# Seven accumulating transfers a head, and score tiles in sets of two and three, in a fused attention layer

## The chip, the cores and the metric

The kernel runs on one core of a Trainium2 chip. The metric is the device time of one execution in microseconds (us). All data are float32, held in HBM at the start and at the end.

## The reference

A layer norm feeds two branches whose results are added to the input: multi-head attention with biases, and three matrix products followed by a tanh. There are 4 sequences of 2048 tokens and 512 channels; attention has 16 heads of 32 channels, so 64 (sequence, head) pairs, called heads here.

```python
B, S, DIM, H = 4, 2048, 512, 16
def attention(xn):
    q = split_heads(xn @ q_w.T + q_b, H) / sqrt(DIM // H)
    k = split_heads(xn @ k_w.T + k_b, H)
    v = split_heads(xn @ v_w.T + v_b, H)
    attn = softmax(einsum('bhqd,bhkd->bhqk', q, k))      # 2048 x 2048 per head
    ctx = merge_heads(einsum('bhqk,bhkd->bhqd', attn, v))
    return ctx @ out_w.T + out_b
def ffn(xn):
    return tanh(xn @ weight @ aux_weight1 @ aux_weight2 + ffn_bias)
out = x + attention(layernorm(x)) + ffn(layernorm(x))
```

## The kernel before

**Stages.** `build_weights` and `build_project` prepare and project the tokens and leave q, k (each split in a high and a low part), v and the tanh branch in HBM. `build_attend` runs the 64 heads one after another, in a loop of four heads a turn whose last four heads are written out, and then the output projection. The change is in `build_attend` alone.

**One head on TensorE (PE).** The scores of a head are computed twice. The first time (`max_scores`, into `sm_bank`, line 926) they give the row maxima: 64 units, each a 128 x 512 block. The second time (`scores`, into `st_bank`, line 942) they are laid out keys by queries, with the maximum folded in as an extra row: 16 key tiles `kt`, each 128 x 2048 and in four units. `both_scores` interleaves the two unit by unit, the maxima belonging to the next head: tile `kt` goes with the maxima units 4(kt+4) to 4(kt+4)+3 of the next head, and tiles 12 to 15 with the units 0 to 15 of the head after that. `use` multiplies a finished tile of probabilities with v (`pv_bank`, line 948), four matmuls a tile. The order is written out by hand in pairs of tiles: scores of tiles 2p and 2p+1, then `use` of the pair before. `turn_max` (line 935) transposes the 16 columns of maxima and stands before unit 8, that is before tile 14. `add_up` (also line 948, into `sm_bank`) sums the head's probability total over its partitions with a matrix of ones. It is written after the scores of tile 9 of the next head, and waits until all of that head's transfers into `dma_sum` have landed.

**Banks.** The maxima have 4 PSUM banks and the `st_bank` scores 3, so PE can be four maxima units ahead of VectorE (DVE) and three score units ahead of ScalarE (ACT). `st_slot` leaves a place out before units 22 (tile 5) and 44 (tile 11): these two wait for the unit two before them.

**ACT** takes the exponential of every score unit (`exps`, line 762) into one of eight `probs` buffers, tile 0 straight into `dma_sum`; it also copies `pv_bank` and the sums (line 769) and issues the next loads of q, k and v.

**DVE** reduces every maxima unit (line 846), turns the transposed maxima round (line 828), reduces the 64 partial maxima (line 863) and takes the reciprocal of the sums of the head before in pieces (line 838), placed after the maxima units named in `RECIPS`.

**GpSimd (POOL)** adds up probability tiles. Nine of its instructions a head (`add`, line 697) sum the ten tiles 1, 3, 4, 6, 7, 9, 11, 12, 14, 15 into `pool_sum`. The tiles 2, 5, 8, 10 and 13 are added onto tile 0 in `dma_sum` by accumulating DMAs that POOL issues (`join`, line 708), each of which waits until the one before has landed. A sixth one (`merge`, line 716) adds `pool_sum` to `dma_sum`. `scale` (line 722) multiplies the context by the reciprocals. POOL's order for a head is written by hand: join of tile 2, the first add, then the merge of the head before, the other adds with the joins of tiles 5, 8, 10 and 13 behind the adds 1, 3, 5 and 7, then `scale` of the head before, and the ninth add.

In the texts below "join 2" is the join of tile 2, and so on, and "sums" is PE's `add_up`.

Of the kernel before, what the change touches and what calls it, by code (L numbers as in the profile page):

```python
# [40 lines left out]
RECIPS = [63, 7, 15]  # L41
CUT = 10
LOAD_AT = [6, 7, 9, 10, 12, 13, 15]
# [4 lines left out]
POOL_TILES = [kt for kt in range(KT) if not any(kt in tiles for tiles in CHAINS)]  # L48
# [4 lines left out]
SCALE_ADD = 8  # L53
# [467 lines left out]
def build_attend(nc, dram, out, first):  # L521

    with ExitStack() as own:
# [27 lines left out]
        join_due, joined = sem("join_due"), [sem("joined0"), sem("joined1")]  # L553
        pool_added, sums_ready, recip_ready, context_ready = sem("pool_added"), sem("sums_ready"), sem("recip_ready"), sem("context_ready")
# [121 lines left out]
        def _(pool):  # L676
# [33 lines left out]

            def merge(h, r):

                pool.wait_ge(pool_added, PRIME + h * POOL_ADDS + POOL_ADDS)
                pool.wait_ge(joined[r % 2], landed(h, len(CHAINS[0]) - 1))
                pool.sem_inc(join_due, 1)
                nc.gpsimd.dma_start(dma_sum[r % 2][:], pool_sum[r % 2][:], accum_op=ALU.add).then_inc(joined[r % 2], DMA)
# [14 lines left out]
            for i in range(POOL_ADDS):  # L731
                sum_up(0, 0, i)

            def body(h, r, more, following):
                for i in range(POOL_ADDS):
                    if i == SCALE_ADD:
                        scale(h, r)
                    if more >= 1:
                        sum_up(following, (r + 1) % GROUP, i)
                    if i == MERGE_AFTER:  # L740
                        merge(h, r)

# [3 lines left out]
        def _(act):  # L746
# [3 lines left out]
            def exps(h, r, kt):  # L750

                for q in range(QB):
                    if q == 0 and kt in SLOT:
                        old, back = tile_before(kt)
                        act.wait_ge(tile_used, PRIME + h * KT - back * KT + old + 1)
                        if old in POOL_TILES:
                            act.wait_ge(pool_added, PRIME + h * POOL_ADDS - back * POOL_ADDS + adds_after(old))
                        elif old != kt and not (back and isinstance(h, int) and h == 0):
                            before, place = (h - 1, (r + 1) % 2) if back else (h, r % 2)
                            act.wait_ge(joined[place], landed(before, CHAINS[0].index(old)))  # L760
# [148 lines left out]
        def _(pe):  # L909
# [79 lines left out]
            for p in range(CUT // 2):  # L989
                both_scores(0, 0, 2 * p, 1, 2)  # L990
                both_scores(0, 0, 2 * p + 1, 1, 2)
                if p:
                    use(0, 0, 2 * p - 2)
                    use(0, 0, 2 * p - 1)

            def body(h, r, more, following, to_turn):
                r1 = (r + 1) % GROUP
                for p in range(CUT // 2, KT // 2):
                    both_scores(h, r, 2 * p, to_turn, more)
                    both_scores(h, r, 2 * p + 1, to_turn, more)  # L1000
                    use(h, r, 2 * p - 2)
                    use(h, r, 2 * p - 1)
                if more >= 1:
                    for p in range(CUT // 2):
                        both_scores(following, r1, 2 * p, to_turn + 1, more - 1)
                        both_scores(following, r1, 2 * p + 1, to_turn + 1, more - 1)
                        if p == 0:
                            use(h, r, KT - 2)
                            use(h, r, KT - 1)
                        else:  # L1010
                            use(following, r1, 2 * p - 2)
                            use(following, r1, 2 * p - 1)
                        if p == CUT // 2 - 1:
                            add_up(h, r, more)
                else:
                    use(h, r, KT - 2)
                    use(h, r, KT - 1)
# [72 lines left out]
```

## Time and profile before

| | us |
|---|---|
| median of 3 runs (lowest, highest) | 4178.22 (4175.97, 4180.62) |
| the profiled execution, its own time | 4178.57 |
| its span in the trace | 4176.8 |
| PE busy | 4086.4 (98%) |
| POOL busy | 3251.6 (78%) |
| DVE busy | 3110.1 (74%) |
| ACT busy | 2360.6 (57%) |
| `scale` of the first head starts | 948.2 |
| `scale` of the last head starts | 4006.9 |

The share of the whole span says little, since the heads are only the part from about 900 to 4010 us. PE, POOL and the DMA engines all have to be read there, head by head. Matmuls are pipelined, and the profile models their ends: a busy PE need not be a PE at its peak, so its time is read from the distance of the starts.

### The profile page before, as it was taken

The page shows a single profiled execution, that of the slowest core. Times are in us where ns is not written, and L with a number is a line of the kernel's source. Part 1 is how long each engine was busy: PE and PEld are TensorE (multiplying, and loading weights), DVE is VectorE, ACT ScalarE, POOL GpSimd, SP SyncE. Part 2 cuts the span into 40 slices and gives each one's busy share as a digit, 9 for nine tenths or more (in the row PEclk, how much of TensorE's full clock was granted, in tenths as well). Part 3 has the DMA queues.
Part 4 walks back from the last instruction along what each step waited for, and adds up shares of the span by engine and source line. Part 5 has one row for each costly group of instructions (what it writes and reads, how often), then busy time and mean ns, then how long its engine had stood idle before and what let it go on. Part 6 is the DMA issues. An engine that isn't in the chain of part 4 may idle for free.

```text
span 4176.8 us, 77708 instructions
## 1 busy us (share of the span) xinstructions
PE 4086.4 (98%) x21216; PEld 2490.0 (60%) x21216; DVE 3110.1 (74%) x5056; ACT 2360.6 (57%) x4517; POOL 3251.6 (78%) x1183
## 2 busy tenths in 40 slices
PE   8999999899999999999999999999999999999989
PEld 6888888655555555555555555555555555555467
DVE  4443334588888888888888888888888888888444
ACT  2221222166666666666666666666666667666621
POOL 1222222279999999999999999999999999999920
PEclk9999999999999999999999999999999999999999
DMA  4444445368788888888888888888888888887777
GB/s 169 163 162 158 151 161 170 132 139 170 166 177 175 179 170 174 171 173 172 175 177 173 175 171 167 172 175 177 176 171 172 173 173 175 176 178 163 167 248 250
DMA packets 246256, 722.11 MB, mean 173 GB/s; under 512 B 87296, under 2 KB 88320, under 8 KB 184448
## 3 DMA queue, kind: packets, MB, share of 16 engines
q0 software_dynamic: 55296, 402.68, 49.8%
q1 hardware_dynamic: 107552, 201.88, 14.2%
q10 hardware_dynamic: 83040, 113.01, 9.7%
q8 instruction: 185, 3.03, 0.3%
q14 instruction: 183, 1.50, 0.1%
HBM read 178.00 MB, written 136.31 MB: 75 GB/s over the span
## 4 chain that ended last, share of the span: by engine, by line
PE 48%; DMA 18%; issue 9%; ACT 3%; POOL 2%; POOLq 0%; DVE 0%; ACTq 0%; SPq 0%; DVEq 0%
PE sm_bank L926 14%; PE st_bank L942 14%; PE pv_bank L948 14%; DMA dma_sum<-pool_sum 10%; DMA dma_sum<-probs 7%; PE sm_bank L235 3%; ACT probs L762 3%; PE sm_bank L948 1%; POOL pool_sum L697 1%; PE st_bank L235 1%; POOL ctx_out L722 1%; POOL dma_sum L708 0%; PE sm_bank L935 0%; ACTq L761 0%; DMA k_stack<-s_k_hi 0%
## 5 line engine op out<-in xcount | busy, mean ns | idle before, releaser
L846 DVE TENSOR_REDUCE part_max<-sm_bank 128x1 f32<-128x512 f32 x4032 | 2450.4, 677 | 413.8 <-PE sm_bank L926 407.4
L697 POOL TENSOR_TENSOR pool_sum<-pool_sum,probs 128x2048 f32<-128x2048 f32 x512 | 2503.2, 4889 | 18.1 <-ACT probs L762 2.2
L762 ACT ACTIVATE probs<-st_bank 128x512 f32<-128x512 f32 x3840 | 1959.3, 614 | 610.5 <-PE st_bank L942 577.7
L926 PE MATMUL sm_bank<-k_stack,q_stack 96*128 96x512 f32 x4032 | 1663.0, 413 | 4.4 <-issue 2.7
L942 PE MATMUL st_bank<-q_stack,k_stack 97*128 97x512 f32 x4096 | 1647.1, 403 | 14.8 <-ACT probs L762 8.5
L926 PEld LDWEIGHTS sm_bank<-k_stack,q_stack 96*128 96x128 f32 x4032 | 767.2, 190 | 558.8 <-DVE part_max L846 339.0
L942 PEld LDWEIGHTS st_bank<-q_stack,k_stack 97*128 97x128 f32 x4096 | 778.6, 190 | 271.4 <-ACT probs L762 127.6
L948 PE MATMUL pv_bank<-probs,v_pair 128*32 128x512 f32 x7680 | 937.6, 603 | 0.0
L948 PEld LDWEIGHTS pv_bank<-probs,v_pair 128*32 128x32 f32 x7680 | 204.9, 109 | 457.3 <-ACT probs L762 264.0
L708 POOL DMA_DIRECT2D dma_sum<-probs x320 | 349.3, 1092 | 80.3 <-ACT probs L762 35.2
L349 POOL TENSOR_TENSOR y_out<-y_out,x_in 128x512 f32<-128x512 f32 x64 | 82.7, 1292 | 385.7 <-ACT y_out L378 379.9
L697 POOL TENSOR_TENSOR pool_sum<-probs 128x2048 f32<-128x2048 f32 x64 | 330.5, 5164 | 0.1
L838 DVE RECIPROCAL ratio<-sum_copy 128x168 f32<-128x168 f32 (+1 forms) x192 | 230.5, 1202 | 42.3 <-ACT sum_copy L769 42.3
L372 ACT ACTIVATE qk_hi<-proj,qk_bias 128x512 fp32r<-128x512 f32 x128 | 88.3, 690 | 271.3 <-PE proj L235 271.3
L431 DVE SCALAR_TENSOR_TENSOR qk_lo<-proj,qk_bias,qk_hi 128x512 fp32r<-128x512 f32 x128 | 96.1, 751 | 194.8 <-ACT qk_hi L372 193.0
L378 ACT ACTIVATE y_out<-y_out 128x512 f32<-128x512 f32 x64 | 40.5, 633 | 333.0 <-DVE y_out L457 333.0
L762 ACT ACTIVATE dma_sum<-st_bank 128x512 f32<-128x512 f32 x256 | 132.5, 602 | 146.5 <-PE st_bank L942 146.5
L235 PE MATMUL proj<-xt_hi,w_hi 128*128 128x512 f32 x512 | 202.9, 396 | 2.2 <-DVEq L461 2.2
L235 PE MATMUL proj<-w_hi,xt_lo 128*128 128x512 f32 x512 | 204.0, 398 | 0.0
L235 PE MATMUL proj<-xt_hi,w_lo 128*128 128x512 f32 x512 | 203.0, 396 | 0.0
L235 PE MATMUL proj<-xt_lo,w_hi 128*128 128x512 f32 x512 | 202.8, 396 | 0.0
L235 PE MATMUL proj<-w_hi,xt_hi 128*128 128x512 f32 x512 | 202.3, 395 | 0.0
(100 smaller groups left out, 2401.6 us busy)
## 6 DMA issues: line engine op xcount, KB each, us to landing
dma_sum<-probs POOLq DMA_DIRECT2D x320, 1024.0 KB, 8.3
dma_sum<-pool_sum POOLq DMA_DIRECT2D x64, 1024.0 KB, 10.3
q_stack<-s_q_hi ACTq DMA_DIRECT2D x122, 256.0 KB, 5.6
k_stack<-s_k_hi ACTq DMA_DIRECT2D x122, 256.0 KB, 4.4
x_in<-in_x SPq DMA_DIRECT2D x16, 1024.0 KB, 7.7
s_q_hi<-qk_hi SPq DMA_DIRECT2D x16, 1024.0 KB, 4.3
s_q_lo<-qk_lo SPq DMA_DIRECT2D x16, 1024.0 KB, 6.5
s_k_hi<-qk_hi SPq DMA_DIRECT2D x16, 1024.0 KB, 4.3
```

Of the source, the lines that this page charges most:

```text
L235: last = nc.tensor.matmul(out, a(c), b(c), start=(c == 0 and n == 0), stop=(c == CT - 1 and n == 2))
L349: nc.gpsimd.tensor_tensor(y_out[:, j], y_out[:, j], x_in[par][:, j], ALU.add).then_inc(half_y, 1)
L372: nc.scalar.activation(qk_hi[:, t, g], proj[:, u % RING], ACT.Identity, bias=keep["qk_bias"][:, t, g:g + 1]).then_inc(hi_ready, 1)
L431: nc.vector.scalar_tensor_tensor(qk_lo[:, t, g], proj[:, u % RING], keep["qk_bias"][:, t, g:g + 1], qk_hi[:, t, g].bitcast(F32), ALU.add, ...
L697: nc.gpsimd.tensor_tensor(total[:], one[:], tile_at(r, kt)[:], ALU.add).then_inc(pool_added, 1)
L708: nc.gpsimd.dma_start(dma_sum[r % 2][:], tile_at(r, CHAINS[0][j])[:], accum_op=ALU.add).then_inc(joined[r % 2], DMA)
L762: nc.scalar.activation(tile_at(r, kt)[:, q * BLK:(q + 1) * BLK], st_bank[:, st_place(kt * QB + q)], ACT.Exp, scale=SCALE).then_inc(probs_r ...
L838: nc.vector.reciprocal(ratio[:, columns], sum_copy[r % 2][:, columns]).then_inc(recip_ready, 1)
L846: nc.vector.tensor_reduce(part_max[:, k:k + 1], sm_bank[:, sm_place(k)], AX.X, ALU.max).then_inc(max_scores_read, 1)
L926: nc.tensor.matmul(sm_bank[:, sm_place(k)], q_st[r][0:ROWS, q * P:(q + 1) * P], k_st[r][0:ROWS, b * BLK:(b + 1) * BLK], start=True, stop=T ...
L942: nc.tensor.matmul(st_bank[:, st_place(u)], k_st[r][0:ROWS + 1, kt * P:(kt + 1) * P], q_st[r][0:ROWS + 1, q * BLK:(q + 1) * BLK], start=Tr ...
L948: last = nc.tensor.matmul(bank[q * DH:(q + 1) * DH, :], left, right[:, q * BLK:(q + 1) * BLK], start=start, stop=stop)
```

## The change

- **The last tile.** Tile 15 is no longer among POOL's tiles, so there are eight adds a head. In its place `top_up` issues an accumulating DMA of tile 15 onto `pool_sum`, with semaphores of its own (`topped`), once the head's adds are done and the tile is there. `merge` waits for `topped` and not for the last add. ACT waits for `topped` before it fills the buffer of tile 15 again, with tile 7 of the next head.
- **POOL's order.** `scale` stands behind all adds of the next head, and `top_up` of the next head behind `scale`.
- **PE's order.** Six sets of 2, 2, 3, 3, 3, 3 tiles in place of eight pairs; `add_up` is still behind the scores of tile 9. `turn_max` now falls inside the last set.
- **The reciprocal** in two pieces of 256 columns, behind the maxima units 3 and 15, in place of three of 168, 168 and 176 behind 63, 7 and 15.

```diff
-RECIPS = [63, 7, 15]
+RECIPS = [3, 15]
+SETS = [(0, 1), (2, 3), (4, 5, 6), (7, 8, 9), (10, 11, 12), (13, 14, 15)]
+CUT_SET = 4
...
-POOL_TILES = [kt for kt in range(KT) if not any(kt in tiles for tiles in CHAINS)]
+TOP = KT - 1
+POOL_TILES = [kt for kt in range(TOP) if not any(kt in tiles for tiles in CHAINS)]
...
+            def top_up(h, r):
+
+                pool.wait_ge(probs_ready, PRIME + h * UNITS + QB * (TOP + 1))
+                pool.wait_ge(pool_added, PRIME + h * POOL_ADDS + POOL_ADDS)
+                pool.sem_inc(join_due, 1)
+                nc.gpsimd.dma_start(pool_sum[r % 2][:], tile_at(r, TOP)[:], accum_op=ALU.add).then_inc(topped[r % 2], DMA)
+
             def merge(h, r):
 
-                pool.wait_ge(pool_added, PRIME + h * POOL_ADDS + POOL_ADDS)
+                pool.wait_ge(topped[r % 2], (h // 2) * DMA + DMA)
                 pool.wait_ge(joined[r % 2], landed(h, len(CHAINS[0]) - 1))
...
             def body(h, r, more, following):
                 for i in range(POOL_ADDS):
-                    if i == SCALE_ADD:
-                        scale(h, r)
                     if more >= 1:
                         sum_up(following, (r + 1) % GROUP, i)
                     if i == MERGE_AFTER:
                         merge(h, r)
+                scale(h, r)
+                if more >= 1:
+                    top_up(following, (r + 1) % GROUP)
...
+                        elif old == TOP and not (isinstance(h, int) and h == 0):
+                            act.wait_ge(topped[(r + 1) % 2], ((h - 1) // 2) * DMA + DMA)
...
             def body(h, r, more, following, to_turn):
                 r1 = (r + 1) % GROUP
-                for p in range(CUT // 2, KT // 2):
-                    both_scores(h, r, 2 * p, to_turn, more)
-                    both_scores(h, r, 2 * p + 1, to_turn, more)
-                    use(h, r, 2 * p - 2)
-                    use(h, r, 2 * p - 1)
+                for g in range(CUT_SET, len(SETS)):
+                    for kt in SETS[g]:
+                        both_scores(h, r, kt, to_turn, more)
+                    for kt in SETS[g - 1]:
+                        use(h, r, kt)
                 if more >= 1:
-                    for p in range(CUT // 2):
...
+                    for g in range(CUT_SET):
+                        for kt in SETS[g]:
+                            both_scores(following, r1, kt, to_turn + 1, more - 1)
+                        for kt in SETS[g - 1]:
+                            use(following if g else h, r1 if g else r, kt)
+                    add_up(h, r, more)
```

On POOL, from the join of tile 13 of one head to the join of tile 5 of the next, before:

```order
L708 DMA dma_sum<-probs 128x2048
...
L722 TENSOR_TENSOR ctx_out<-pv_copy,ratio 128x512
...
L697 TENSOR_TENSOR pool_sum<-pool_sum,probs 128x2048
...
L708 DMA dma_sum<-probs 128x2048
...
L697 TENSOR_TENSOR pool_sum<-probs 128x2048
...
L716 DMA dma_sum<-pool_sum 128x2048
...
L697 TENSOR_TENSOR pool_sum<-pool_sum,probs 128x2048
...
L708 DMA dma_sum<-probs 128x2048
```

And the same stretch now:

```order
L712 DMA dma_sum<-probs 128x2048
...
L733 TENSOR_TENSOR ctx_out<-pv_copy,ratio 128x512
...
L720 DMA pool_sum<-probs 128x2048
...
L712 DMA dma_sum<-probs 128x2048
...
L701 TENSOR_TENSOR pool_sum<-probs 128x2048
...
L727 DMA dma_sum<-pool_sum 128x2048
...
L701 TENSOR_TENSOR pool_sum<-pool_sum,probs 128x2048
...
L712 DMA dma_sum<-probs 128x2048
```

Where an add of about one tile stood between join 13 and join 2, there is now only the issue of a transfer (L720), and what the merge (L727) waits for has become that transfer.

On PE, in the last head, which has no maxima beside its scores (a tile of scores is four matmuls, and so is a `use`), from tile 4 on. Before:

```order
L942 MATMUL st_bank<-q_stack,k_stack 128x512 x8
L948 MATMUL pv_bank<-probs,v_pair 32x512 x8
L948 MATMUL sm_bank<-dma_sum,ones_att 32x512 x4
L942 MATMUL st_bank<-q_stack,k_stack 128x512 x8
L948 MATMUL pv_bank<-probs,v_pair 32x512 x8
```

Now:

```order
L957 MATMUL st_bank<-q_stack,k_stack 128x512 x12
L963 MATMUL pv_bank<-probs,v_pair 32x512 x12
L963 MATMUL sm_bank<-dma_sum,ones_att 32x512 x4
L957 MATMUL st_bank<-q_stack,k_stack 128x512 x12
L963 MATMUL pv_bank<-probs,v_pair 32x512 x12
```

The sums stay where they were; around them PE changes between scores and `use` after twelve matmuls where it did after eight.

On DVE, in the head before the last, from its maxima unit 16 to the end of what accompanies tile 15. Before:

```order
L846 TENSOR_REDUCE part_max<-sm_bank 128x1 x48
L838 RECIPROCAL ratio<-sum_copy 128x168
L863 TENSOR_REDUCE row_max<-part_max 128x16
L846 TENSOR_REDUCE part_max<-sm_bank 128x1 x8
L838 RECIPROCAL ratio<-sum_copy 128x168
L828 TENSOR_SCALAR max_row<-sm_bank 16x128
L846 TENSOR_REDUCE part_max<-sm_bank 128x1 x8
L838 RECIPROCAL ratio<-sum_copy 128x176
```

Now:

```order
L861 TENSOR_REDUCE part_max<-sm_bank 128x1 x48
L878 TENSOR_REDUCE row_max<-part_max 128x16
L861 TENSOR_REDUCE part_max<-sm_bank 128x1 x4
L853 RECIPROCAL ratio<-sum_copy 128x256
L861 TENSOR_REDUCE part_max<-sm_bank 128x1 x4
L843 TENSOR_SCALAR max_row<-sm_bank 16x128
L861 TENSOR_REDUCE part_max<-sm_bank 128x1 x8
L853 RECIPROCAL ratio<-sum_copy 128x256
```

The two pieces stand where the sets (10, 11, 12) and (13, 14, 15) end, and `max_row` has twelve reductions around it with no change of PE to `use` between.

## Rows read from the trace of the kernel before

**Rows 1.** The page: busy time by engine, DMA share in 40 slices.

```profile
PE 4086.4 (98%) x21216; PEld 2490.0 (60%) x21216; DVE 3110.1 (74%) x5056; ACT 2360.6 (57%) x4517; POOL 3251.6 (78%) x1183
DMA  4444445368788888888888888888888888887777
```

**Rows 2.** POOL's timeline (start us, us, engine, line), one head and its surroundings.

```profile
2413.66 0.89 POOL L708 DMA_DIRECT2D dma_sum<-probs  x1
2414.28 1.59 POOL L722 TENSOR_TENSOR ctx_out<-pv_copy,ratio 128x512 f32<-128x512 f32 x1
2415.54 4.88 POOL L697 TENSOR_TENSOR pool_sum<-pool_sum,probs 128x2048 f32<-128x2048 f32 x1
2420.08 1.19 POOL L708 DMA_DIRECT2D dma_sum<-probs  x1
2420.70 5.20 POOL L697 TENSOR_TENSOR pool_sum<-probs 128x2048 f32<-128x2048 f32 x1
2425.22 1.52 POOL L716 DMA_DIRECT2D dma_sum<-pool_sum  x1
2430.51 1.70 POOL L708 DMA_DIRECT2D dma_sum<-probs  x1
...
2442.19 0.88 POOL L708 DMA_DIRECT2D dma_sum<-probs  x1 [0.72 <-ACT probs L762]
...
2462.86 0.88 POOL L708 DMA_DIRECT2D dma_sum<-probs  x1 [0.37 <-ACT probs L762]
```

**Rows 3.** DMA issues of 2413 to 2421 us: count, KB, us to landing.

```profile
dma_sum<-probs POOLq DMA_DIRECT2D x2, 1024.0 KB, 7.4
```

**Rows 4.** The same of 2425.0 to 2426.5 us.

```profile
dma_sum<-pool_sum POOLq DMA_DIRECT2D x1, 1024.0 KB, 10.9
```

**Rows 5.** The same of 2430.3 to 2431.5 us.

```profile
dma_sum<-probs POOLq DMA_DIRECT2D x1, 1024.0 KB, 11.1
```

**Rows 6.** DMA of 2405 to 2454 us: GB/s in 40 slices of 1.225 us.

```profile
GB/s 214 214 214 214 0 13 0 0 207 221 214 214 166 162 214 214 214 181 234 221 221 201 227 274 227 214 140 301 54 207 13 107 214 214 214 107 294 139 1 107
```

**Rows 7.** Scale on POOL over all heads: duration ns, first and last start.

```profile
L722 POOL TENSOR_TENSOR ctx_out<-pv_copy,ratio x64: 1540/1578/3152, 948.2 to 4006.9; 128x512 f32<-128x512 f32 x64
```

**Rows 8.** PE's timeline: a change to use, one back, and the sums.

```profile
2408.86 0.40 PE L942 MATMUL st_bank<-q_stack,k_stack 97*128 97x512 f32 x1
2409.10 0.47 PE L926 MATMUL sm_bank<-k_stack,q_stack 96*128 96x512 f32 x1
2409.41 0.39 PE L942 MATMUL st_bank<-q_stack,k_stack 97*128 97x512 f32 x1
2409.73 1.92 PE L948 MATMUL pv_bank<-probs,v_pair 128*32 128x512 f32 x16
2411.58 0.50 PE L926 MATMUL sm_bank<-k_stack,q_stack 96*128 96x512 f32 x1
2411.92 0.40 PE L942 MATMUL st_bank<-q_stack,k_stack 97*128 97x512 f32 x1
...
2433.33 1.92 PE L948 MATMUL pv_bank<-probs,v_pair 128*32 128x512 f32 x16
2436.20 1.07 PE L948 MATMUL sm_bank<-dma_sum,ones_att 128*32 128x512 f32 x8 [0.94 <-DMA dma_sum<-pool_sum]
2437.19 0.50 PE L926 MATMUL sm_bank<-k_stack,q_stack 96*128 96x512 f32 x1
```

**Rows 9.** DVE's timeline: reductions, and the pieces of the reciprocal.

```profile
2399.42 1.19 DVE L838 RECIPROCAL ratio<-sum_copy 128x168 f32<-128x168 f32 x1
2400.53 0.22 DVE L828 TENSOR_SCALAR max_row<-sm_bank 16x128 fp32r<-16x128 f32 x1
2400.67 4.85 DVE L846 TENSOR_REDUCE part_max<-sm_bank 128x1 f32<-128x512 f32 x8
2405.45 1.23 DVE L838 RECIPROCAL ratio<-sum_copy 128x176 f32<-128x176 f32 x1
2412.12 4.87 DVE L846 TENSOR_REDUCE part_max<-sm_bank 128x1 f32<-128x512 f32 x8 [0.72 <-PE sm_bank L926]
```

More of the change, by code:

```diff
@@ L52 @@
 SLOT = {kt: i % 7 for i, kt in enumerate([*range(1, 13), 14, 15])} | {13: 7}
-SCALE_ADD = 8
 RESULT_TILES = [9, 11]
@@ L553, in build_attend @@
         join_due, joined = sem("join_due"), [sem("joined0"), sem("joined1")]
+        topped = [sem("topped0"), sem("topped1")]
         pool_added, sums_ready, recip_ready, context_ready = sem("pool_added"), sem("sums_ready"), sem("recip_ready"), sem("context_ready")
@@ L732, in _ @@
                 sum_up(0, 0, i)
+            top_up(0, 0)
             def body(h, r, more, following):
                 for i in range(POOL_ADDS):
-                    if i == SCALE_ADD:
-                        scale(h, r)
                     if more >= 1:
@@ L988, in _ @@
                 max_scores(1, 1, k)
-            for p in range(CUT // 2):
[L990 to L994, printed above, removed]
+            for g in range(CUT_SET):
+                for kt in SETS[g]:
+                    both_scores(0, 0, kt, 1, 2)
+                for kt in SETS[g - 1] if g else ():
+                    use(0, 0, kt)
             def body(h, r, more, following, to_turn):
                 r1 = (r + 1) % GROUP
-                for p in range(CUT // 2, KT // 2):
-                    both_scores(h, r, 2 * p, to_turn, more)
-                    both_scores(h, r, 2 * p + 1, to_turn, more)
-                    use(h, r, 2 * p - 2)
-                    use(h, r, 2 * p - 1)
-                if more >= 1:
[L1004 to L1014, printed above, removed]
-                else:
-                    use(h, r, KT - 2)
-                    use(h, r, KT - 1)
+                for g in range(CUT_SET, len(SETS)):
[3 more added lines that the diff above has]
+                        use(h, r, kt)
+                if more >= 1:
+                    for g in range(CUT_SET):
+                        for kt in SETS[g]:
+                            both_scores(following, r1, kt, to_turn + 1, more - 1)
+                        for kt in SETS[g - 1]:
+                            use(following if g else h, r1 if g else r, kt)
+                    add_up(h, r, more)
+                else:
+                    for kt in SETS[-1]:
+                        use(h, r, kt)
             def output(n, par, ahead):
```

## The prediction

> **What bounds the kernel now.** Start with the page's busy shares and the DMA line [rows 1]: PE at 98% looks like the bound, but in the heads, from the tenth slice on, the DMA engines are busy for 70 to 80% and more as well. The share does not tell which of them sets the length of a head. POOL's timeline does [rows 2]. Call J the issue of join 13 (2413.66). Then come the last add at J+1.88, join 2 at J+6.42, the merge at J+11.56, join 5 at J+16.85, join 8 at J+28.53 and, with join 10 between, the next join 13 20.67 later: 49.20 us for the head. POOL stands idle in only two places, 0.72 before join 8 and 0.37 before the next join 13, so 48.11 of the 49.20 is POOL's own work. The mean head is (4006.9 - 948.2) / 63 = 48.55 us [rows 7].
>
> The 0.72 is ascribed to ACT, but join 5 was issued at 2430.51 and landed 11.1 later, at 2441.61 [rows 5], and join 8, which must wait for it, followed 0.58 later. The reader is to see that the loop is POOL's work plus one DMA wait. Leaving the 0.37 out, the same sum for this head is 48.83, so it runs 0.28 above the mean, and I compare with 48.83.
>
> PE is second, and close: its use of the pair before the sums begins at 2433.33 and takes 1.85, so it could begin the sums at 2435.18 and begins at 2436.20, the moment when the merge lands (2425.22 + 10.9) [rows 4, 8]. PE needs 49.20 - 1.02 = 48.2 us in this head.
>
> **POOL's work.** One add goes: 2415.54 to 2420.08 is 4.54. One DMA issue comes: 0.62 (2413.66 to 2414.28) to 0.95 (the merge and join 5 stand before adds that end late); 0.7 taken. POOL's own work falls from 48.1 to about 44.3. Moving scale behind the adds costs nothing: it stood behind join 13 before, and stands there now. If nothing else changed, the head would be PE's.
>
> **The new wait.** The merge waited for an add that had ended nearly 5 us before. Now it waits for the seventh transfer, and this is issued at J+1.88, only 1.88 after join 13. Joins 13 and 2, the pair nearest to it, are 6.42 apart and land 7.4 after issue, each as good as alone [rows 2, 3]. Transfers of this kind do not overlap: one alone moves for four slices at 214 GB/s, 4.9 us, with pauses between them; closer ones run on at 200 to 230 GB/s without a pause [rows 6]. The three that are issued 5 us apart land at 2427.48, 2436.12 and 2441.61, 8.64 and 5.49 apart [rows 2 to 5], though nothing but bandwidth ties them. So the seventh lands about 4.9 after join 13: J + 7.4 + 4.9 = J+12.3, which is **10.4 after its own issue**. The ends: 7.4, as if alone, and 14.2, if it takes the merge's 8.64 behind join 13's landing. I take 10.4 because the stores of the context, which follow scale in both kernels, are already in the 7.4 of rows 3.
>
> In the meantime POOL issues join 2 (J+2.6) and does one add (4.52), until J+7.8. Then it waits for the seventh until T = J+12.3: **4.5 us idle**, on the engine that bounds the loop, with six more adds queued behind it.
>
> **The second wait grows.** The merge is issued at T+0.6 (the 0.58 between join 5's landing and join 8) and join 5 5.29 later, at T+5.9. Join 2 was issued long before, but its bytes only start when the seventh's end; it lands at T+4.9. If the merge and join 5 land 8.64 and 5.49 behind it, as now, join 8 can go at T+19.6. If nothing queued, POOL's work alone would bring it at T + 5.9 + 10.96 = T+16.9. I take 18.9, nearer to the first, since it is the same transfers and loads of q and k that compete; the slices in which the merge moves go down to 140 and 54 GB/s, so not all of its 8.64 is queue.
>
> **Sum of the loop.** 1.88 (join 13 and scale) + 10.4 (seventh) + 18.9 (to join 8) + 20.3 (20.67 less the 0.37) = **51.5 us**, against 48.83: +2.7. In the loop's 63 distances the first has no full queue, so 62 x 2.7 = +167.
>
> **PE's order.** Two changes between scores and use go. One costs 0.32 - 0.24 going in, 1.85 - 2 x 0.86 = 0.13 inside (a tile is 0.86, the two of 1.85 less the one of the sums, 0.99), and 0.34 - 0.24 coming back [rows 8]: 0.31, so -0.62 a head. Against it stands the ring of four maxima banks. In a set PE writes a maxima unit every 0.47 and DVE reads one in 0.60 (2400.67 to 2405.45, eight), starting 0.54 behind [rows 8, 9]. Unit k waits for the end of unit k-4, which is at 0.54 + 0.60 (k - 3) + 0.1; PE reaches it at 0.1 + 0.47 k. In pairs (k up to 7) it just holds; in threes, k = 11 is 0.2 late, 0.3 with the restart. This falls on (7, 8, 9). In (4, 5, 6) and (10, 11, 12) the units 22 and 44 hold PE anyway, which covers it. In (13, 14, 15) the larger piece of the reciprocal (256/168 x 1.11 = 1.7) makes DVE start some 0.3 later (12 x 0.60 + 1.7 = 8.9, against PE's 24 x 0.235 + 0.3 + 2.7 = 8.6), and max_row lies between: 0.7. Less 0.1 that pairs lose today, +0.9 at most, +0.7 taken. PE needs 48.2 - 0.6 + 0.7 = 48.3, with both ends 47.9 and 48.6. All of it hides under POOL's 51.5 and costs nothing, as long as the loop is POOL's. The reciprocal's pieces are 3.4 us in all either way and wait for sums that are ready a set of tiles earlier.
>
> ACT's new wait, for tile 7 on the seventh transfer, lies ahead of the sums of the same head. If it comes to anything it takes a part of PE's wait there and adds none: POOL waits for the same landing.
>
> **Total.** Against the profiled execution's own 4178.6 (span 4176.8; the median is 4178.2, so nothing is to be corrected): 4178.6 + 167 = 4346.
>
> **Rivals.**
> 1. *The transfers overlap, and PE sets the length: faster.* If the seventh lands 7.4 after issue and join 5 is no longer waited for, the loop is 1.88 + 7.4 + 16.9 + 20.3 = 46.5, PE's 48.3 is longer, and it gains 48.55 - 48.3 = 0.25, up to 0.65 a head: -15 to -40, 4155. It holds as soon as the seventh's latency and the 16.9 to 19.6 sum to under 26; I have 29.3. For it: POOL is truly relieved by 3.8 us. Against it: the flat 200 to 230 GB/s.
> The Trainium skill, "DMA: Bandwidth & Descriptors", section "Anatomy of one DMA — SWDGE (gpsimd) path", gives 2.0 us plus the bytes at 436 GB/s. By that, an estimate, the seventh would land under 5 us after its issue and this rival would hold. The trace disagrees: 7.4 for 1 MB alone.
> 2. *Only the first wait comes.* Seventh 10.4, but join 5 lands in time: 49.5, +0.7 a head, 4220; spread 4175 to 4265. For it: the merge's 8.64 contains loads that could fall elsewhere.
> 3. *The queue backs up further.* Seventh at 14.2: 55 and more, above 4440. Against it: nothing in the stretch before join 2 moves much but the 256 KB of stores.
>
> **How the numbers follow.** The forecast's own spread is a loop of 50.2 to 53.0, that is +1.4 to +4.2, 4265 to 4439: chance 0.71. Rival 1: 0.12. Rival 2: 0.12. Rival 3: 0.05. Range 4185 to 4440: it leaves out rival 1, rival 3 and the bottom of rival 2. Within 0.2% (8 us, about what a measurement can tell) lie 0.02 of rival 1 and 0.02 of rival 2: 0.04. Faster: 0.10 of rival 1 and 0.01 of rival 2, 0.11. Slower: 0.85.
>
> **What would show it.** In POOL's timeline after: the merge 12 to 13 us behind join 13's issue with some 4.5 idle before it; join 8 over 12.5 behind join 5, with an idle time that a DMA ends. In the DMA issues: the seventh landing at 10 to 11, join 5 at 12 or more. On PE: a wait of 2 to 3.5 before the sums in every head. It is wrong if POOL waits for ACT's tiles rather than for DMAs, if the seventh lands in under 8, or if PE's wait at the sums is gone.

## The result and the profile after

The changed kernel takes 4473.9 us (median of 4 runs, 4472.9 to 4475.6) against 4179.4 for the kernel before in the same runs: ratio 1.0709, 95% interval 1.0695 to 1.0722. It is slower by 294 us, or 4.7 us for each of the 63 steps from head to head. The direction was forecast, the size was not: 4346 was predicted, and the range ended at 4440. Some executions of any of these kernels ran slow as a whole; a kernel's time in this text is the median of the others.

Busy time by engine, and the DMA share in 40 slices, from the page of the changed kernel, beside [rows 1]:

```profile
PE 4196.0 (94%) x21216; PEld 2517.7 (56%) x21216; DVE 3130.0 (70%) x4992; ACT 2386.2 (53%) x4517; POOL 3015.3 (67%) x1183
DMA  4444445488888888888888888888888888888787
```

POOL does 236 us less and PE is idle more. What became longer is a wait. POOL's timeline of the changed kernel, from join 13 to the next one (start us, us, engine, line, idle before), beside [rows 2]:

```profile
2450.17 0.85 POOL L712 DMA_DIRECT2D dma_sum<-probs  x1
2450.78 1.56 POOL L733 TENSOR_TENSOR ctx_out<-pv_copy,ratio 128x512 f32<-128x512 f32 x1
2452.01 1.19 POOL L720 DMA_DIRECT2D pool_sum<-probs  x1
2454.75 0.87 POOL L712 DMA_DIRECT2D dma_sum<-probs  x1 [1.55 <-PE pv_bank L963]
2455.32 4.91 POOL L701 TENSOR_TENSOR pool_sum<-probs 128x2048 f32<-128x2048 f32 x1
2464.70 0.88 POOL L727 DMA_DIRECT2D dma_sum<-pool_sum  x1 [4.46 <-DMA pool_sum<-probs]
2465.32 4.88 POOL L701 TENSOR_TENSOR pool_sum<-pool_sum,probs 128x2048 f32<-128x2048 f32 x1
2470.68 0.88 POOL L712 DMA_DIRECT2D dma_sum<-probs  x1 [0.48 <-issue]
2471.30 9.47 POOL L701 TENSOR_TENSOR pool_sum<-pool_sum,probs 128x2048 f32<-128x2048 f32 x2
2483.17 0.88 POOL L712 DMA_DIRECT2D dma_sum<-probs  x1 [2.40 <-ACT probs L777]
...
2493.30 0.89 POOL L712 DMA_DIRECT2D dma_sum<-probs  x1
...
2503.39 0.88 POOL L712 DMA_DIRECT2D dma_sum<-probs  x1
```

Where POOL had two short waits in this stretch of its loop, 0.72 and 0.37, it now has four: before join 2 (1.55), before the merge (4.46, for the seventh transfer), before join 5 (0.48) and before join 8 (2.40). When the transfers issued at 2450.17, 2452.01, 2454.75, 2464.70 and 2470.68 landed is in five answers on the DMA issues of these moments, in this order (the last column is us from issue to landing), beside [rows 3 to 5]:

```profile
dma_sum<-probs POOLq DMA_DIRECT2D x1, 1024.0 KB, 8.4
pool_sum<-probs POOLq DMA_DIRECT2D x1, 1024.0 KB, 12.0
dma_sum<-probs POOLq DMA_DIRECT2D x1, 1024.0 KB, 15.4
dma_sum<-pool_sum POOLq DMA_DIRECT2D x1, 1024.0 KB, 12.7
dma_sum<-probs POOLq DMA_DIRECT2D x1, 1024.0 KB, 11.9
```

So they land at 2458.6, 2464.0, 2470.2, 2477.4 and 2482.6: one every 5 to 7 us, though the first three were issued within 5 us. The seventh, at 2464.0, lets the merge go at 2464.7. Join 2, at 2470.2, lets join 5 go at 2470.7; the profile calls this wait "issue", but join 5 may not go before join 2 has landed. Join 5, at 2482.6, lets join 8 go at 2483.2; the profile names ACT there, but in the mean too join 8 goes 0.6 after join 5 has landed.

This is one head. POOL's waits over all heads (us in total, times, longest) show the same places with another split: in the mean 3.5 us before join 2, for PE's use of tile 0, and 2.5 before the merge.

```profile
POOL dma_sum L712 <- PE pv_bank L963: 217.7, 62, 7.1
POOL dma_sum L727 <- DMA pool_sum<-probs: 149.3, 50, 12.3
```

The same distances, averaged over 60 heads of each trace (worked out from POOL's timeline and the DMA issues, us; predicted in the last column):

| from | to | before | after | predicted |
|---|---|---|---|---|
| join 13 | merge | 11.55 | 14.49 | 12.9 |
| merge | join 5 | 5.28 | 6.46 | 5.3 |
| join 5 | join 8 | 11.59 | 12.16 | 13.0 |
| join 8 | next join 13 | 20.38 | 20.37 | 20.3 |
| **a head** | | **48.80** | **53.48** | **51.5** |
| issue to landing | join 13 | 7.6 | 7.6 | 7.4 |
| | seventh | | 11.8 | 10.4 |
| | join 2 | 7.9 | 13.7 | |
| | merge | 10.2 | 12.6 | |
| | join 5 | 11.0 | 11.6 | |

63 times 4.68 is 295 us, the whole result. PE waits for POOL's loop before the sums, 2.1 us each time in 57 heads:

```profile
PE sm_bank L963 <- DMA dma_sum<-pool_sum: 120.4, 57, 6.5
```

(who waited for whom on PE: us in total, times, longest). There is a second wait on PE's side. ACT's tile 9 takes the `probs` buffer of tile 2, and so waits until join 2 has landed:

```profile
2470.22 1.58 ACT L777 ACTIVATE probs<-st_bank 128x512 f32<-128x512 f32 x3 [2.04 <-DMA dma_sum<-probs]
```

With ACT held, the scores of the set (7, 8, 9) take PE 1.3 us longer in the mean than in e4 below, where nothing of the kind is waited for. Both waits lie within what PE has to spare. TensorE's granted clock in the heads falls from 1.00 to 0.97 or 0.98 of 2.4 GHz in the windows of 500 us, with PE waiting more. A set without such a wait is no longer for it ((13, 14, 15) is 6.31 us here and in e4), so I take the clock for a follower; no run holds it fixed.

### The profile page after: what moved, and what is told of

It is laid out like the page before. It is cut to its first block and busy times, and to the rows that moved or that the text cites. A ratio compares the mean times of both kernels' runs of the same rounds, so it can differ in the third digit from the quotient of the medians.

```text
span 4473.8 us, 77764 instructions
## 1 busy us (share of the span) xinstructions
PE 4196.0 (94%) x21216; PEld 2517.7 (56%) x21216; DVE 3130.0 (70%) x4992; ACT 2386.2 (53%) x4517; POOL 3015.3 (67%) x1183
## 5 line engine op out<-in xcount | busy, mean ns | idle before, releaser
L777 ACT ACTIVATE probs<-st_bank 128x512 f32<-128x512 f32 x3840 | 1985.5, 610 | 584.2 <-PE st_bank L957 465.4
L701 POOL TENSOR_TENSOR pool_sum<-pool_sum,probs 128x2048 f32<-128x2048 f32 x448 | 2131.4, 4758 | 16.8 <-ACT probs L777 1.0
L957 PE MATMUL st_bank<-q_stack,k_stack 97*128 97x512 f32 x4096 | 1677.7, 411 | 85.2 <-ACT probs L777 77.7
L941 PE MATMUL sm_bank<-k_stack,q_stack 96*128 96x512 f32 x4032 | 1717.1, 427 | 26.7 <-DVE part_max L861 25.4
L957 PEld LDWEIGHTS st_bank<-q_stack,k_stack 97*128 97x128 f32 x4096 | 794.6, 194 | 348.2 <-ACT probs L777 207.9
L963 PE MATMUL pv_bank<-probs,v_pair 128*32 128x512 f32 x7680 | 932.5, 614 | 0.0
L712 POOL DMA_DIRECT2D dma_sum<-probs x320 | 284.6, 889 | 448.9 <-PE pv_bank L963 250.7
L963 PEld LDWEIGHTS pv_bank<-probs,v_pair 128*32 128x32 f32 x7680 | 221.7, 112 | 515.4 <-issue 291.1
L701 POOL TENSOR_TENSOR pool_sum<-probs 128x2048 f32<-128x2048 f32 x64 | 314.8, 4918 | 4.5 <-ACT probs L777 4.4
L853 DVE RECIPROCAL ratio<-sum_copy 128x256 f32<-128x256 f32 x128 | 222.1, 1736 | 48.8 <-ACT sum_copy L784 48.8
L784 ACT ACTIVATE sum_copy<-sm_bank 128x512 f32<-128x512 f32 x64 | 38.2, 597 | 363.3 <-PE sm_bank L963 363.3
## 6 DMA issues: line engine op xcount, KB each, us to landing
dma_sum<-pool_sum POOLq DMA_DIRECT2D x64, 1024.0 KB, 12.6
```

Source lines behind the costliest of these rows:

```text
L701: nc.gpsimd.tensor_tensor(total[:], one[:], tile_at(r, kt)[:], ALU.add).then_inc(pool_added, 1)
L712: nc.gpsimd.dma_start(dma_sum[r % 2][:], tile_at(r, CHAINS[0][j])[:], accum_op=ALU.add).then_inc(joined[r % 2], DMA)
L777: nc.scalar.activation(tile_at(r, kt)[:, q * BLK:(q + 1) * BLK], st_bank[:, st_place(kt * QB + q)], ACT.Exp, scale=SCALE).then_inc(probs_r ...
L853: nc.vector.reciprocal(ratio[:, columns], sum_copy[r % 2][:, columns]).then_inc(recip_ready, 1)
L941: nc.tensor.matmul(sm_bank[:, sm_place(k)], q_st[r][0:ROWS, q * P:(q + 1) * P], k_st[r][0:ROWS, b * BLK:(b + 1) * BLK], start=True, stop=T ...
L957: nc.tensor.matmul(st_bank[:, st_place(u)], k_st[r][0:ROWS + 1, kt * P:(kt + 1) * P], q_st[r][0:ROWS + 1, q * BLK:(q + 1) * BLK], start=Tr ...
```

## The experiments

Two theories. **L** (called W in the expectations of e1 to e4): the seventh transfer stands in a queue whose landings POOL waits for one after the other; the latency in that loop is the price, and PE's order is hidden. **P**: PE's new order costs a good part. Later a third, **T**: the DMA engines are short of throughput over a head as a whole, wherever the transfer is put.

### Each part alone

e1_seventh_only: the change without PE's sets and without the two-piece reciprocal.

```diff
-RECIPS = [3, 15]
+RECIPS = [63, 7, 15]
...
-                for g in range(CUT_SET, len(SETS)):
+                for p in range(CUT // 2, KT // 2):
```

> The seventh transfer and POOL's order as in the change, but PE in pairs and the reciprocal in its three old pieces. Theory W (the merge's wait for the seventh transfer, and the queue behind it, set the head; PE's order is hidden): 53 to 54 us a head, 4440 to 4480 us, within 20 us of the changed kernel. Rival P (PE's sets of three cost a good part of the 294 us, through the four maxima banks or through a later use of tile 0): 51 us a head or less, 4330 us or less.

4470.7 us, 1.0696 (1.0677 to 1.0715). The seventh transfer, with POOL's order, is the whole loss: 53.5 us a head, 14.6 from join 13 to the merge. P is out.

e2_sets_only: the kernel before with the other half (PE's loops go over `SETS` as in the change).

```diff
-RECIPS = [63, 7, 15]
+RECIPS = [3, 15]
+SETS = [(0, 1), (2, 3), (4, 5, 6), (7, 8, 9), (10, 11, 12), (13, 14, 15)]
```

> PE's sets and the two pieces of the reciprocal alone; POOL adds tile 15 itself, as before, and there are six transfers a head. Theory W: POOL's loop of 48.8 us stays the bound and PE needs 48.3, so 4170 to 4200 us. Rival P: over 4230 us.

4211.8 us, 1.0080 (1.0062 to 1.0098): slower by 31 us, over the 4170 to 4200 expected and under P's 4230. PE's sets and the two pieces are not free. Beside the seventh this is hidden, as e1 shows, but by themselves they are a loss. A head takes 49.3 us; e4 shows that PE's new order explains 49.0 of it, and the rest stays open.

e4_no_seventh: the change without `top_up`; the merge waits for the eighth add. Tile 15 is left out of the sums.

```diff
-                pool.wait_ge(topped[r % 2], (h // 2) * DMA + DMA)
+                pool.wait_ge(pool_added, PRIME + h * POOL_ADDS + POOL_ADDS)
...
                 scale(h, r)
-                if more >= 1:
-                    top_up(following, (r + 1) % GROUP)
```

> The changed kernel without the seventh transfer; the merge waits for the eighth add, and tile 15 is left out of the sums. PE's sets stay. This shows what PE needs in its new order when POOL is relieved. Theory W: 48.2 to 48.4 us a head, 4140 to 4165 us, no wait of PE at the sums. Rival P: over 4200 us.

4194.7 us, 1.0032 (1.0009 to 1.0056), where 4140 to 4165 was expected. PE does not wait at the sums and needs 48.98 us a head (the shortest quarter of the heads), not 48.3. By the prediction's arithmetic a set of three takes 5.9 us (24 matmuls at 0.235 and 0.3) plus what its waits add. In this trace (7, 8, 9) takes 6.14, (13, 14, 15) 6.31, and (4, 5, 6), with a place left out of the `st_bank` ring, 6.18. But (10, 11, 12), with such a place as well, takes 7.05. PE's timeline in that set:

```profile
2447.50 0.39 PE L938 MATMUL sm_bank<-k_stack,q_stack 96*128 96x512 f32 x1
2447.73 0.39 PE L954 MATMUL st_bank<-q_stack,k_stack 97*128 97x512 f32 x1
2448.45 0.50 PE L938 MATMUL sm_bank<-k_stack,q_stack 96*128 96x512 f32 x1 [0.34 <-DVE part_max L858]
```

The matmul that starts 0.72 after the one before it is maxima unit 0. The ring of four banks ends with two places left out (`SM_TURN` ends in `None, None`), so unit 0 takes the bank of unit 62, two units back, not four. In pairs that seam, the place where the ring starts anew, lay under the use of tiles 8 and 9. In (10, 11, 12) it lies inside the set, and 0.9 us is what this set takes over (4, 5, 6).

e5_pairs_no_seventh: e4 with PE in pairs and the reciprocal in three pieces (tile 15 is again left out of the sums).

> As the changed kernel without the seventh transfer (tile 15 is left out of the sums), but PE in pairs and the reciprocal in three pieces. Theory R (in the set (10, 11, 12) maxima unit 0 comes behind unit 63, and its bank is that of unit 62, two units before, since the ring leaves two places out there; in pairs this seam lies under the use of tiles): the 0.9 us that this set takes over its due is gone, PE needs 48.2 us a head in place of 48.98: 4135 to 4160 us against 4195. Rival (threes as such cost it, by DVE's pace): within 15 us of 4195.

4172.0 us, 0.9982 (0.9972 to 0.9991), where 4135 to 4160 was expected. PE's unhindered head is 48.1 us in this trace (the shortest quarter of them), against 48.98. That fits the seam, but does not isolate it: this run also has two more changes between scores and `use`, and the old pieces of the reciprocal. The mean head is 48.7, since the merge now lands after 12.4 and join 5 after 13.0; I put this to the loads, which meet an earlier POOL in the queue, but no run tests it. Relieving POOL of an add is worth about 8 us here, with the add's work left out altogether and the loads where they were.

### How much of it is the bytes, and where they stand

e3_seventh_short and e7_seventh_half: the seventh moves 128 or 1024 of 2048 columns; the rest of tile 15 is left out of the sums.

```diff
-                nc.gpsimd.dma_start(pool_sum[r % 2][:], tile_at(r, TOP)[:], accum_op=ALU.add).then_inc(topped[r % 2], DMA)
+                nc.gpsimd.dma_start(pool_sum[r % 2][:, 0:128], tile_at(r, TOP)[:, 0:128], accum_op=ALU.add).then_inc(topped[r % 2], DMA)
```

> The changed kernel, but the seventh transfer moves only 128 of the 2048 columns (the rest of tile 15 is left out of the sums). All waits and all orders are those of the change. Theory W in its bandwidth form (the seventh costs by the bytes that it moves behind join 13): it still lands after join 13, at about 6 to 7 us from its issue, the merge goes 9 us behind join 13, and PE's 48.3 us sets the head: 4140 to 4190 us. Rival O (it is the order of waits, whatever the size): over 4300 us.

> The changed kernel with a seventh transfer of 1024 of the 2048 columns (half of tile 15 is left out of the sums). With 128 columns it lands 6.4 us after its issue and the kernel takes 4197 us, with 2048 columns 11.8 us and 4474. Theory L (latency in a loop, hidden until it passes what PE needs): it lands after 8.9 us, the loop is 50.0 us against PE's 48.98, 4240 to 4280 us. Rival B (every byte costs the same): 4335 us.

4197.2 and 4334.7 us, ratios 1.0044 (1.0029 to 1.0059) and 1.0375 (1.0354 to 1.0396). The waits by themselves, with hardly a byte, cost 2.5 us over e4, and 4140 to 4190 was missed as it was in e4. Then the columns cost about the same all the way: 138 us from 128 to 1024 of them and 139 for the second half. My 4240 to 4280 for the half was wrong, and the rival figure, 4335, was right. The DMA issues of e3, e7 and the change, in this order, over the heads:

```profile
pool_sum<-probs POOLq DMA_DIRECT2D x62, 64.0 KB, 6.3
```

```profile
pool_sum<-probs POOLq DMA_DIRECT2D x60, 512.0 KB, 9.2
```

```profile
pool_sum<-probs POOLq DMA_DIRECT2D x57, 1024.0 KB, 11.7
```

The latency of the half was near what was expected (9.2 against 8.9). What I had missed is that nothing was left to hide it: at 128 columns the loop is already at 49.1 us (10.92 + 5.24 + 12.56 + 20.39), with join 8 waiting for join 5's landing and PE's 48.98 level with it. With the half the merge goes 1.4 later behind join 13, and join 5 waits for join 2 besides (6.05 behind the merge in place of 5.24): 2.2 us a head, or 138 in all.

e8_join2_short: the full seventh, but join 2 moves 128 columns; most of tile 2 is left out of the sums. The bytes of a head are those of the kernel before, but for 64 KB.

```diff
+                n = 128 if j == 1 else SEQ
-                nc.gpsimd.dma_start(dma_sum[r % 2][:], tile_at(r, CHAINS[0][j])[:],
+                nc.gpsimd.dma_start(dma_sum[r % 2][:, 0:n], tile_at(r, CHAINS[0][j])[:, 0:n],
```

> The changed kernel with its full seventh transfer, but join 2 moves 128 of 2048 columns (most of tile 2 is left out of the sums): as many bytes a head as before, all waits and orders those of the change. Theory L (what counts is what stands in the queue behind join 13 when the merge and join 5 want it): the seventh still lands after 11.8 us, the merge still goes 14.5 us behind join 13, but join 5 no longer waits for join 2: 52.2 us a head, 4380 to 4410 us. Rival T (the DMA engines are short of throughput over the head as a whole, seven megabytes where six went): back to 4200 to 4230 us.

4320.5 us, 1.0339 (1.0321 to 1.0356), neither L's 4380 to 4410 nor T's 4200 to 4230. T does not explain the loss: with hardly more bytes than before the kernel is still 140 us slower. But the other half of the 294 us goes with the bytes of join 2, which stands right behind the seventh. The merge still goes 14.7 behind join 13, and join 5 now follows at 5.16. I had missed that join 5, with less ahead of it, also lands sooner: join 8 follows it at 10.7, not 12.2.

e11_extra_in_gap and e12_extra_behind_join13: the kernel before with 45 extra transfers of 1024 KB between two idle buffers, in one place or the other. The buffers are set to zero at the start, and what is loaded into them later waits for the last extra.

```diff
+            def extra(h, r):
+
+                if r:
+                    pool.wait_ge(extra_landed, (h // GROUP) * (3 * DMA) + r * DMA)
+                if r < 3:
+                    pool.sem_inc(join_due, 1)
+                    nc.gpsimd.dma_start(wo_hi[:].bitcast(F32), wo_lo[:].bitcast(F32),
+                                        accum_op=ALU.add).then_inc(extra_landed, DMA)
...
+                    if i == 4 and more == GROUP:
+                        extra(h, r)
```

(`i == 7` in e12.)

> The kernel before with one more accumulating DMA of 1024 KB in three of four heads of the loop (45 in all), from one idle buffer onto another, so that nobody waits for its data. POOL issues it behind the add of tile 9, half way between join 8 and join 10, where the queue runs empty. Theory L (an extra transfer costs what it delays, and here it delays nothing that is waited for): POOL's issue alone, 0.6 to 0.9 us in 45 heads, 4205 to 4225 us. Rival T (short of throughput over the head): as much as the same transfer behind join 13.

> The same 45 extra transfers, but issued directly behind join 13, in front of join 2, the merge and join 5. Nobody waits for them. Theory L: join 2, the merge and join 5 land 2 to 2.5 us later after their issue, join 8 waits that much longer: 2.6 us in 45 heads, 4280 to 4310 us. Rival T: as much as in the gap.

4267.5 and 4414.8 us, ratios 1.0211 (1.0193 to 1.0230) and 1.0554 (1.0530 to 1.0578): 1.9 us a transfer in the gap, 5.2 behind join 13. The place is worth a factor of 2.7, for a transfer nobody waits for. Both cost more than I gave them. POOL's timeline of e12:

```profile
2425.84 0.87 POOL L713 DMA_DIRECT2D dma_sum<-probs  x1
2426.43 1.18 POOL L735 DMA_DIRECT2D wo_hi_sb<-wo_lo_sb  x1
...
2432.79 1.53 POOL L713 DMA_DIRECT2D dma_sum<-probs  x1
...
2437.94 1.85 POOL L721 DMA_DIRECT2D dma_sum<-pool_sum  x1
...
2447.69 0.88 POOL L713 DMA_DIRECT2D dma_sum<-probs  x1 [3.26 <-DMA dma_sum<-probs]
```

Join 2, issued at 2432.79, lands 14.3 later (2447.1), and join 5 waits 3.26 for it. It is the wait that the prediction left out, here without any seventh transfer. In the gap the extra makes join 10 land after 10.6 us in the mean and up to 12.2, where it was 8.1 before, and in 12 heads join 13 waits 1.4 to 2.1 for it: there is a gap, but not of 5 us.

### What stretches the landings

The seventh lands 6.1 us behind join 13, where 4.9 was reckoned. Two kinds of traffic stand beside it: SP's stores of the context (256 KB a head, issued when `scale` is done) and ACT's loads.

e16_seventh_before_scale issues it 1.25 us sooner, ahead of the stores of the context.

```diff
+                if more >= 1:
+                    top_up(following, (r + 1) % GROUP)
                 scale(h, r)
-                if more >= 1:
-                    top_up(following, (r + 1) % GROUP)
```

> The changed kernel with the seventh transfer issued ahead of scale and not behind it, 1.25 us sooner, and ahead of the four stores of the context (256 KB), which SP issues when scale is done. The changed kernel's seventh lands 6.1 us behind join 13. If 1.2 of that are the stores, it now lands 5 us behind it, the merge goes 13.3 us behind join 13 in place of 14.5, and a head falls by 1.2 us: 4390 to 4415 us. If transfers one behind the other are 6.1 us apart by themselves, nothing changes: 4465 to 4480 us.

4478.4 us, 1.0712 (1.0693 to 1.0731): nothing changes, and the merge goes 14.5 behind join 13 as before. That was no verdict on the stores: issued first is not served first, as the next run shows.

e17_stores_late takes the stores out of that time: SP holds them back until PE has used tile 8 of the head after the next, some 30 us later.

```diff
+                if late:
+                    sp.wait_ge(tile_used, PRIME + h * KT + 2 * KT + 8)
...
-                store(h, r)
+                store(h, r, more >= 2)
```

> The changed kernel, but SP holds the four stores of a head's context (256 KB) back until PE has used tile 8 of the head after the next, some 30 us later. In the changed kernel the seventh lands 6.1 us behind join 13, and it did so too when it was issued ahead of the stores, since the stores and it share the DMA engines whichever is issued first. If the stores are the 1.2 us over the 4.9 of one transfer, the merge now goes 13.3 us behind join 13 in place of 14.5, and a head falls by 1 to 1.5 us: 4380 to 4415 us. If not, 4460 to 4480 us.

4399.8 us, 1.0536 (1.0518 to 1.0554), 74 us less than the change. The merge goes 13.2 behind join 13 (13.3 expected), and the seventh lands after 10.4, 5.1 behind join 13: the very figure predicted, once the 256 KB of stores are not beside it. POOL's timeline of e17:

```profile
2413.83 0.86 POOL L714 DMA_DIRECT2D dma_sum<-probs  x1
...
2415.68 1.19 POOL L722 DMA_DIRECT2D pool_sum<-probs  x1
...
2426.52 0.88 POOL L729 DMA_DIRECT2D dma_sum<-pool_sum  x1 [2.43 <-DMA pool_sum<-probs]
```

e15_change_loads_later moves ACT's loads of q, k and v away instead, and e18_stores_late_loads_later does both.

```diff
-LOAD_AT = [6, 7, 9, 10, 12, 13, 15]
+LOAD_AT = [9, 10, 11, 12, 13, 14, 15]
```

> The changed kernel with ACT's loads moved to behind the tiles 9, 10, 11, 12, 13, 14, 15, as in e13_loads_later. If the loads are a part of what makes the seventh transfer dear (merge and join 5 share the engines with them), join 5 lands 1 to 1.5 us sooner after its issue and a head falls by as much: 4370 to 4410 us. It does not come near the kernel before, since the seventh and join 2 stand in the queue before any load. Rival: the loads play no part here, 4460 to 4480 us.

> Both at once: the stores held back, and ACT's loads behind the tiles 9 to 15 as in e15_change_loads_later (4394 us). If everything that shares the DMA engines with the seventh, join 2, the merge and join 5 counts by its bytes, the gains add up: 4310 to 4340 us, still above the kernel before by 130 us or more, which is then the seventh transfer by itself.

4394.0 us, 1.0507 (1.0488 to 1.0526), and 4309.4 us, 1.0323 (1.0304 to 1.0341). 80 and 74 us singly, 165 together: they add up, and a little more. In e15 join 5 lands after 10.9 (11.6 in the change), the merge after 10.7 (12.6), and join 2 lands 5.5 behind the seventh (6.6). With both, 130 us are left over the kernel before. That is not yet the price of the seventh with neither beside it, since the later loads make the kernel before faster too, as the next run shows: over that one (4142) it is 167 us, or 2.6 a head.

### A version that beats both

The kernel before had the same wait in small: join 8 for join 5, 0.6 us a head. So the loads were moved there too.

> The kernel before with ACT's seven loads of the later head moved from behind the tiles 6, 7, 9, 10, 12, 13, 15 to behind 9, 10, 11, 12, 13, 14, 15, away from the time in which the merge and join 5 move. Theory L: the merge's 10.2 us and join 5's 11.0 from issue to landing shrink by 1 us or more, join 8 no longer waits, POOL's 48.1 us and PE's 48.2 remain: 4140 to 4160 us. Rival: the loads only meet the other joins, and nothing changes: 4175 to 4185.

e13_loads_later, the kernel before with that one line: **4142.2 us, 0.9905 (0.9890 to 0.9921)**. Join 5 lands after 9.6 in place of 11.0, and join 8 follows join 5 after 11.0 in place of 11.6. What is left of POOL's waits for a join, over all heads:

```profile
POOL dma_sum L708 <- ACT probs L762: 6.6, 12, 1.7
POOL dma_sum L708 <- DMA dma_sum<-probs: 2.3, 3, 0.9
```

It was 35.2 and 12.7 us in the kernel before. Then PE's order becomes worth something:

```diff
+SETS = [(0, 1), (2, 3), (4, 5, 6), (7, 8, 9), (10, 11), (12, 13), (14, 15)]
```

> The kernel before with PE in seven sets, (0, 1), (2, 3), (4, 5, 6), (7, 8, 9), (10, 11), (12, 13), (14, 15): one change between scores and use less, and no seam of the ring inside a set. The reciprocal stays in three pieces, POOL and its six transfers stay as before. If the kernel before is bound by POOL's loop with join 5's landing (48.8 us a head), nothing changes: 4170 to 4190 us, and PE waits 0.2 to 0.3 us longer at the sums. If it is bound by PE, 0.3 us a head are won: 4155 to 4162 us.

> The same loads with PE in the seven sets (0, 1), (2, 3), (4, 5, 6), (7, 8, 9), (10, 11), (12, 13), (14, 15). If the later loads free POOL's loop from the DMA, PE's 48.0 us in place of 48.2 may show a little: 4130 to 4160 us, not slower than e13_loads_later. If POOL's loop still waits for join 5, 4170 to 4200.

e9_seven_sets, these sets without the later loads: 4198.9 us, 1.0040 (1.0027 to 1.0053). PE's unhindered head is 47.98, 1.0 under e4's with the seam out of the set, and yet the kernel is slower (4170 to 4190 was expected): the loop is POOL's, join 8 goes 11.85 behind join 5 (11.59 before), and PE only waits longer at the sums. Why join 5 lands 0.2 later in it stays open.

e14_loads_later_seven_sets, both: **4134.6 us, 0.9888 (0.9872 to 0.9904)**, a gain of 47 us. POOL's timeline has no wait left in the head shown, and the merge lands after 8.3 in place of 10.3:

```profile
2409.07 1.67 POOL L710 DMA_DIRECT2D dma_sum<-probs  x1
2409.99 10.02 POOL L699 TENSOR_TENSOR pool_sum<-pool_sum,probs 128x2048 f32<-128x2048 f32 x2
2419.96 0.86 POOL L710 DMA_DIRECT2D dma_sum<-probs  x1
```

```profile
dma_sum<-pool_sum POOLq DMA_DIRECT2D x63, 1024.0 KB, 8.3
```

(timeline of one head, and DMA issues of all heads.) POOL's 48.09 us and PE's 47.98 are now level. PE's order is worth the 8 us between e13 and e14.

## Why the prediction was right and wrong

J is the issue of join 13 and T the landing of the seventh, as in the prediction.

- **What bounds the kernel.** Right. The loop of POOL with join 5's landing was 48.80 us in the mean, and moving seven loads, which touches neither POOL's nor PE's work, freed it of the wait and made the kernel 39 us faster (e13).
- **The relief of POOL is lost.** Right, and more than lost. 4.5 us of idle before the merge were predicted; that 4.46 are in the head shown is chance, for the mean is 2.5, with 3.5 more in front of join 2, which now waits for PE's use of tile 0 (L963). I had it issued at J+2.6; in the mean it goes at J+6.5. POOL's lag behind PE, which had covered that wait, was gone. It costs nothing while the seventh lands later still: in e1 join 2 goes at J+5.6 and lands at J+20.2, in the change at J+6.5 and J+20.3. (Seven adds stand behind the merge, not six; nothing hangs on it.)
- **The seventh's latency.** Mis-sized: 10.4 predicted, 11.8 measured. The step that failed is "the stores of the context are already in the 7.4 of rows 3". They came beside join 13 when the queue ran empty behind it; now the queue does not run empty, and they add their bytes. The stores themselves take longer too, 4.5 us before and 8.5 now:

```profile
s_ctx<-ctx_out SPq DMA_DIRECT2D x252, 64.0 KB, 4.5
```

```profile
s_ctx<-ctx_out SPq DMA_DIRECT2D x228, 64.0 KB, 8.5
```

With the stores moved away, e17 gives the 10.4.

- **The second wait.** Wrong in its parts. "Join 5 5.29 later" left out that join 5 waits for join 2. I had join 2 land at T+4.9, before join 5's turn at T+5.9; it is T+6.6, and join 5 goes 1.2 later. The loads are 1.1 of the 1.7 (T+5.5 in e15); that the merge, issued at T+0.8, takes the rest is not shown by any run. From join 5 to join 8 it is then 12.2, not 13.0. Together T to join 8 is 19.4 against 18.9. The sum of the queue had given 19.6, and one reason to go below it was a misreading of rows 6: the slices at 140 and 54 GB/s begin after 2436.8, when the merge had landed, and in the merge's own slices it is 201 to 274.
- **The sum.** +1.4 (seventh), +0.2 (0.8, not 0.6, from landing to the merge), +1.2, -0.8: 53.5 instead of 51.5. In 63 steps these 2.0 us are 126 of the 128 us between 4346 and the result. The range ended at a loop of 53.0; its upper end should have held join 2's landing and the stores, both of which could be read in the code and in rows 2 to 6.
- **PE's order.** Hidden, as said (e1 against the change: 3 us). Its price was wrong: 48.98 us and not 48.3, with 0.9 from the seam at unit 0, which the prediction leaves out though it has the same kind of place at units 22 and 44 of the other ring. This price would have decided rival 1: PE in six sets is slower than the old loop (e2, e4). ACT's wait on the seventh came to little, as said (some 10 us in all); its wait on join 2, before tile 9, was not foreseen.
- **Rival 1** could not come true: even with no seventh transfer at all the change is at 4195. **Rival 2** would have needed join 2 and join 5 to land in time. **Rival 3** had the stretch in which the result lies, at a chance of 0.05, but not by its own means: the seventh lands after 11.8, not 14.2. It named the right direction, a queue that backs up further, and the stores that it then dismissed as too small.
- **The signs.** The merge was to go 12 to 13 behind join 13 (14.5), the seventh to land at 10 to 11 (11.8), join 5 at 12 or more (11.6), join 8 to go over 12.5 behind join 5 (12.2), and PE to wait 2 to 3.5 in every head (2.1, in 57 heads). All name the right place, and all but the last miss the size.
- **The skill's figure.** The estimate in rival 1 from the Trainium skill, "DMA: Bandwidth & Descriptors", "Anatomy of one DMA — SWDGE (gpsimd) path", under 5 us for the seventh, is not borne out: it is 6.3 us for 64 KB in e3, behind join 13, and 11.8 for all of it.

## What to carry to other kernels

Before moving work from an engine to its DMA queue, write down every wait of that engine for a landing, and what stands in the queue when each is due; a transfer costs what it delays there, and loads and stores of other engines count by their bytes. When an engine is relieved, ask which waits its lateness had been covering. Where buffers go round in a ring, look up in the code where the ring skips a place before moving the boundaries of a schedule.

## What the runs showed of the hardware

- Accumulating transfers of 1024 KB issued within less than 5 us of each other land one after the other: 5.1 us apart without stores or loads among them (join 13 and the seventh in e17), 5.2 to 7.2 in the head of the changed kernel shown above, with them.
- SP's stores and POOL's transfers are not served in the order of their issue: the seventh landed 13.7 us behind join 13's issue whether it was issued behind `scale` or 1.25 us sooner, ahead of the stores, and only taking the stores away helped, to 12.3 (e16, e17). The Trainium skill, "DMA: Bandwidth & Descriptors", section "Queues, rings and completion order", has each DMA engine take turns between its queues packet by packet. The two runs agree as far as they go: issue order did not decide; single packets were not looked at.
- The same 1024 KB cost 1.9 us a head in one place of the queue, 15 us ahead of join 13, and 5.2 in another, 0.6 behind it (e11, e12).
